# Causal attention: the copies of transposed probabilities dealt to VectorE and ScalarE in turn instead of one to two

## The reference

```
q = einsum('bhcq', Q, x) * sq;  k, v likewise      (16 heads of 64)
att = einsum('bhcq,bhCq->bhcC', q, k) / 64
att = where(causal, att, -inf)
p = softmax(att, axis=-1)
y = einsum('bhcC,bhCv->bhcv', p, v)
z = einsum('dvh,bhcv->bcd', W, y) * const
```

## Time and profile before

| what | value |
|---|---|
| median of 3 runs | 2178.86 us (2178.73 to 2180.55) |
| the profiled execution: its time | 2181.41 us |
| its span (first to last instruction) | 2179.6 us |
| TensorE matmuls, busy | 1758.3 us, 81% of the span |
| VectorE, busy | 1469.8 us, 67% |
| ScalarE, busy | 992.0 us, 46% |
| GpSimd, busy | 500.8 us, 23% |
| chain that ended last | TensorE 60%, VectorE 19%, ScalarE 9% |
| copies of pieces by ScalarE (L1599) | 213, 111.0 us |
| copies of pieces by VectorE (L1645) | 107, 67.5 us |
| mean granted clock of TensorE | 0.899 of full |

### The profile page before, as it was taken

One profiled execution on the slowest core, in us unless ns is written; L12 is line 12 of the kernel. 1 busy time (PEld: TensorE's weight loads), 2 busy tenths in 40 slices (PEclk: granted clock), 3 DMA queues, 4 the chain that ended last, 5 costly groups with the idle time before them and its releaser, 6 DMA issues.

```text
span 2179.6 us, 34541 instructions
## 1 busy us (share of the span) xinstructions
PE 1758.3 (81%) x12713; PEld 1265.2 (58%) x12713; DVE 1469.8 (67%) x5012; ACT 992.0 (46%) x2312; POOL 500.8 (23%) x602
## 2 busy tenths in 40 slices
PE   3546666766677877999999999999888999998808
PEld 1335555655564335566666766666657999983306
DVE  3788887787822587677777567776735666753695
ACT  2524334443343753455555345555315445543762
POOL 3011112111120012333333333333302333320002
PEclk9767788878787986999999999999999999999959
DMA  5000000000000011100000000000403333310001
GB/s 153 1 0 1 1 1 1 1 1 1 1 1 1 1 39 24 60 1 1 1 1 1 1 1 2 1 1 2 128 1 88 88 88 78 70 30 0 0 0 39
DMA packets 86314, 49.82 MB, mean 23 GB/s; under 512 B 40205, under 2 KB 83905, under 8 KB 85953
## 3 DMA queue, kind: packets, MB, share of 16 engines
q1 hardware_dynamic: 79361, 47.05, 8.3%
q10 hardware_dynamic: 6784, 0.56, 0.3%
HBM read 45.50 MB, written 2.10 MB: 22 GB/s over the span
## 4 chain that ended last, share of the span: by engine, by line
PE 60%; DVE 19%; ACT 9%; issue 3%; POOL 3%; POOLq 0%; DVEq 0%; ACTq 0%
PE PS L1526 6%; PE PS L1553 6%; PE PS L1824 5%; PE PS L1540 5%; PE PS L713 3%; PE PS L1511 3%; PE PS L1501 3%; DVE sq L667 3%; DVE nx L664 3%; PE PS L719 3%; PE PS L2237 3%; PE PS L1887 2%; PE PS L1568 2%; PE PS L1843 2%; PE PS L1493 2%
## 5 line engine op out<-in xcount | busy, mean ns | idle before, releaser
L1680 POOL TENSOR_SCALAR px<-px,crl 128x128 f32<-128x128 f32 (+7 forms) x128 | 225.9, 1765 | 420.6 <-DVE crl L1652 420.6
L1591 ACT ACTIVATE px<-PS,cnm 128x128 f32<-128x128 f32 (+7 forms) x256 | 189.5, 741 | 265.3 <-DVE cnm L1637 258.5
L182 POOL TENSOR_SCALAR rstd<-mv 128x1 f32<-128x1 f32 x128 | 41.5, 325 | 794.3 <-DVE mv L161 793.6
L667 DVE TENSOR_SCALAR sq<-nx 128x4 f32<-128x4 f32 x1024 | 186.0, 182 | 35.3 <-DVE nx L664 0.2
L664 DVE TENSOR_TENSOR_SCAN nx<-sq 128x6 f32<-128x6 f32 x1024 | 176.2, 172 | 35.5 <-SPq L2304 2.3
L1634 DVE TENSOR_REDUCE cm<-PS 128x1 f32<-128x128 f32 (+6 forms) x224 | 154.2, 689 | 56.9 <-PE PS L1526 56.4
L1540 PE MATMUL PS<-ident,px 128*128 128x128 f32 x1152 | 159.8, 280 | 13.3 <-ACT qT L1579 9.6
L1540 PEld LDWEIGHTS PS<-ident,px 128*128 128x128 f32 x1152 | 131.2, 142 | 60.6 <-issue 35.3
L1526 PE MATMUL PS<-kT,qT 64*128 64x512 f32 (+3 forms) x768 | 158.9, 519 | 4.5 <-ACT px L1591 2.6
L1553 PEld LDWEIGHTS PS<-pT,V 128*64 128x64 f32 x2304 | 124.1, 137 | 64.0 <-issue 34.6
L1553 PE MATMUL PS<-pT,V 128*64 128x128 f32 x2304 | 154.1, 278 | 6.4 <-DVE pT L1645 2.8
(11 more groups left out here) (318 smaller groups left out, 3830.3 us busy)
## 6 DMA issues: line engine op xcount, KB each, us to landing
xbs<-in_fside_Bx16xSxS SPq DMA_DIRECT2D x8, 1232.0 KB, 6.6
fsrc<-in_fside_Bx16xSxS SPq DMA_DIRECT2D x8, 1232.0 KB, 6.6
xmk<-in_mask_Bx16xSxS_bk SPq DMA_DIRECT2D x8, 308.0 KB, 8.5
fsrc<-in_mask_Bx16xSxS_bk SPq DMA_DIRECT2D x8, 308.0 KB, 8.3
X<-in_x SPq DMA_DIRECT2D x1, 2048.0 KB, 11.8
w<-in_L_attn_W_ffn SPq DMA_DIRECT2D x2, 1024.0 KB, 11.9
t<-in_L_ffn_w SPq DMA_DIRECT2D x2, 1024.0 KB, 11.3
out<-xs SPq DMA_DIRECT2D x16, 128.0 KB, 1.7
```

Of the source, the lines that this page charges most:

```text
L667: e.tensor_scalar(o, bass.AP(k.nx, 2, [[6, P], [0, 2], [3, 2]]), 10.0, -10.0, ALU.min, ALU.max).then_inc(sem("rec.clip"), 1)
L1591: e.activation(k.px[n % 2][:, h, 0:width], src, ACT.Exp, scale=-1.0, bias=k.cnm[:, n % 4, h:h + 1], accum_out=k.cl[:, n % 4, h:h + 1]).the ...
L1680: e.tensor_scalar(k.px[n % 2][:, 0, 0:width], k.px[n % 2][:, 0, 0:width], k.crl[:, n % 4, 0:1], None, ALU.mult).then_inc(sem("c.normal0"), 1)
```

## The change

A piece's engine is chosen from the count of all pieces before it. Before, the count modulo 3 gives VectorE for 0 and ScalarE for 1 and 2; after, the count modulo 2 gives VectorE for even and ScalarE for odd. The two programs differ in nothing else; the mask stays in VectorE's instruction of L1637.

```diff
         elif step[0] == "ct":
             for i in range(len(causal_groups(step[2]))):
-                by = min(sum(made) % 3, 1)
+                by = sum(made) % 2
                 made[by] += 1
                 k.piece[step + (i,)] = (("vector", "scalar")[by], made[by], sum(made))
                 ends.append((step + (i,), ("c.pT.vector", "c.pT.scalar")[by], made[by]))
```

## The result

The changed kernel takes 2184.11 us (median of 19 runs, 2182.47 to 2185.89) against 2179.99 us of the kernel before in the same rounds (19 runs, 2178.17 to 2181.54). The ratio is 1.0019, with a 95% interval of 1.0012 to 1.0026: slower by about 4.1 us, between 2.6 and 5.7. It also lies just at the bound of 0.2% that the prediction set for "no change". A second series of the same kernel gave 1.0019 again (1.0009 to 1.0030).

A forecast was written before the change was run, and what follows sets the result against it. TensorE was taken to bound the causal stage, with 25.3 us idle. The terms -0.2 + 1.2 + 1.05 - 0.3 = +1.75 us gave 2183.2 us for a profiled execution, 2180.6 by the median, range 2176.5 to 2185.

The forecast's parts named there:

- The bound: Causal stage: TensorE, busy 658.7 of 684 us, sets the pace; at most its 25.3 us idle can be won.
- Tiles 2 to 7 at 0: Scores of tile 2 to those of tile 7 in each unit: stays 25.65 us, cost 0.
- The three intervals of the pattern: Tile 7 to tile 0, tile 0 to 1, tile 1 to 2: 7.18, 4.32 and 3.10 us in regular units.
- The sum of -0.2: Three intervals from tile 7 to tile 2: average 14.61 before, 14.60 after, over 15 units -0.2 us.
- the three places: Unit 1, and twice in unit 8, where VectorE's first copy comes late: +1.2, +0.55 and +0.5 us.
- (a): Unit 1, transposes of tile 7: VectorE's first copy waits behind its output-weight copies, holding the fourth group, +1.2 us.
- (b): Unit 8, transposes of tiles 6 and 7: VectorE's residual and statistics delay its first copy, +0.55 and +0.5 us.
- (c): End of the last unit: tile 6's last piece goes to ScalarE, VectorE's scaling is sooner done, -0.3 us.
- rival (2): All 53 moved copies are on the path and their longer duration is paid: +5.2 us, 2184.1; chance 5%.
- The ports: Moved copies read PSUM, neither wait for GpSimd nor delay it; otherwise the sum could grow by up to 36 us.
- (1): VectorE's first piece holds the fourth group in many of 32 tiles: 0.55 us each, 8.8 for half, 2187.7; chance 10%.
- (3): ScalarE was the late one; unloading it returns a quarter of 25.3 us idle, -6 us, 2172.9; chance 7%.

The follow-up runs named there:

- mended: Changed kernel with three tiles (tile 7 of unit 0, tiles 6 and 7 of unit 8) copied ScalarE, ScalarE, VectorE, ScalarE; 1.0007, again 1.0002 of the kernel before.
- wzp_moved: Changed kernel with VectorE's two copies rearranging the output weights two tiles later, the weights' transposes moving with them; 0.9999 of the kernel before.
- late_only: Kernel before with only tile 7 of unit 0 and tiles 6 and 7 of unit 8 alternating VectorE, ScalarE; 1.0016 of the kernel before.
- s_first: Changed kernel with the same even split, 160 and 160, begun by ScalarE instead of VectorE; 1.0016 of the kernel before.
- all_scalar: Changed kernel with all 320 pieces copied by ScalarE; 1.0017 of the kernel before.
- ssvs: Changed kernel with tiles 6 and 7 of all units copied ScalarE, ScalarE, VectorE, ScalarE; 0.9990, again 0.9988 of the kernel before.

## Why the prediction was right or wrong

**The bound.** Right in that TensorE sets the stage's pace and late copies cost. "TensorE busy as before" is not what the profile shows: from unit 1 to unit 15 its idle time is 17.29 us before and 17.52 after, and the busy time rose by 2.20, since the short waits of the transposes lie inside their rows.

**Tiles 2 to 7 at 0.** Right in all regular units: 25.65 us. In units 1 and 2 it is 0.12 and 0.11 more, which by the prediction's own last sentence ("moved by over 0.1 us") was a sign of being wrong. It goes with the weights' work beside: `mended` has it too, and with that work moved (`wzp_moved`) the interval is 3.57 again.

**The three intervals of the pattern.** Right within 0.01: 7.18, 4.33, 3.10. The sum of -0.2 agrees with `mended`, whose stage is 0.20 us below before once the three places are gone; this 0.20 already holds the +0.2 of units 1 and 2 named above, so the rest gave back some 0.4.

**(a), +1.2.** Measured 5.53 - 4.27 = +1.26. Shown by taking the piece away (`mended`), by taking away what stands ahead of it (`wzp_moved`) and by adding it alone (`late_only`).

**(b), +0.55 and +0.5.** Measured 11.24 - 10.58 = +0.66 and 8.56 - 7.93 = +0.63. The wait itself is 0.46 and 0.47. The rest fits a term that I had left out: four transposes begun anew take 0.66 us, and at the end of an unbroken row they add only 1.99 - 1.53 = 0.46.

**(c), -0.3.** The wait for VectorE's scaling fell from 1.38 to 1.09 us, as forecast. The end as a whole is only 0.15 us shorter: unit 15's own interval from tile 0 to 1, now with a V first, takes 4.34 us instead of 4.22, and the rest is within 0.05. The row that waited:

```profile
1551.97 2.73 PE L1540 MATMUL PS<-ident,px 128*128 128x128 f32 x16 [1.09 <-DVE px L1656]
```

**The step that failed** is the first section's "The kernel outside this stage is not touched". No instruction there changed, but the clock did: behind the stage +1.6 us in one profile of the changed kernel and +0.4 in the other, and the prediction had no term for it. In the stage the sum was short by some 0.5 us: 2.43 - 0.15 = +2.3 instead of +1.75; the three places cost 2.63 instead of 2.25, and the end gave back 0.15 instead of 0.3. With both, the profiles give 3.9 and 2.6 us where 4.1 (2.6 to 5.7) was timed. By its mechanism the prediction was right, by its size a term was missing. That the time fell into the range is in part luck: the upper end of 2185 came from the spread of the runs and from rival (2), not from a term for the clock. The 79% for "within 0.2%" leaned on the same sum: the ratio of 1.0019 just keeps it, and its interval, up to 1.0026, doesn't.

**The ports.** The moved copies didn't delay GpSimd: its scaling takes 1758 ns in the mean against 1765 before, and VectorE's own scaling 574 ns against 648, since it begins later and waits less for GpSimd's end. From the page of the changed kernel:

```profile
L1680 POOL TENSOR_SCALAR px<-px,crl 128x128 f32<-128x128 f32 (+7 forms) x128 | 225.1, 1758 | 423.1 <-DVE crl L1652 423.1
L1656 DVE TENSOR_SCALAR px<-px,crl 128x128 f32<-128x128 f32 (+7 forms) x128 | 73.5, 574 | 4.5
```

This agrees with what the Trainium skill, "SBUF — State Buffer", "Who interferes with whom", says: a VectorE instruction with at most one input in SBUF, outside the two-port modes, doesn't contend with GpSimd.

**The rivals.** (1), the first piece holding the fourth group, is the mechanism that did cost, but in the three places of the sum and not in half of 32; no regular unit joined. (2), every longer copy paid, named +5.2 us and 2184.1, and 2184.11 was measured; this is chance, for its mechanism is refuted by `mended`, by `late_only` and by the 25.65. (3), idle time given back by unloading ScalarE, is there in part: in `mended`, between units 1 and 15, TensorE's idle time is 15.51 us instead of 17.29, and its busy time, with the longer rows of the transposes, 579.15 instead of 577.57, which leaves the 0.2.

**Open** is what decides how many rows behind the stage run at the lower clock, whether the edit had any part in it, and the 1 to 5 us by which `s_first` was timed above what its profile holds.

## What to carry to other kernels

Where neither copying engine is the bound, an even count of copies is the wrong measure: ask which copy is waited for first (it frees the bank for the group n places later) and which last (the consumer needs all), and give the first to the engine whose queue is empty then and the last so that it doesn't stand behind another copy on the same engine. A rotation that doesn't divide the number of pieces shows several patterns within one trace, and the differences between its intervals priced the new pattern here to 0.01 us in the regular units, where durations times counts, rival (2), had 5.2 us for the exchange. Work that appears only in some rounds (statistics, rearranged weights) must be looked up by place, since it is there that a harmless pattern becomes a wait.

## What was not expected of the hardware

TensorE's granted clock behind the stage changed although neither the instructions nor the waits ahead of the rows did, and in one profile this is worth 1.6 us beside the 2.3 of the stage: a row of 16 projection matmuls takes 3.72 us at the upper level and up to 6.45 (`all_scalar`) with the lower. The same program can differ in this from one execution to the next: in unit 0 the four matmuls of a q projection (L1493) take 3.78 us in one profile of the changed kernel and 1.98 in the other, and with the rows behind them that unit takes 39.27 and 36.49 us. At the end of the last unit the clock can also be a gain: in `ssvs` and `wzp_moved` the transposes and the product with V stay at the upper level (1.00), and the end of the stage is 1.9 and 1.7 us shorter. So differences of a tenth of a per cent can be read in a trace only piece by piece, with the granted clock of each stretch beside it.
